# SyncE's table numbers packed by two, its waits grouped, and a ring of eight y buffers in the expert stage

## The reference

```python
h = embed(x); h = conv31(h) + bias                  # 8 x 512 tokens, 256 channels
h = h + attention(layernorm(h))                     # 16 heads of 64, linear attention
h = h + experts(layernorm(h))
# experts, for 4096 tokens (xf) and 8 experts, four 256 wide and four 512 wide
probs = sigmoid(xf @ router_w.T)
topw, sel = top_k(probs, 2); topw = topw / (topw.sum(-1, keepdims=True) + 1e-20)
h = square(relu(einsum('td,edw->tew', xf, W1e)))
y = einsum('tew,ewd->ted', h, W2e)
out = einsum('ted,te->td', y, combine)              # combine: topw at the two chosen experts
```

## Time and profile before

| | before |
|---|---|
| median of 3 runs | 714.23 us (714.22 to 716.38) |
| the profiled execution | 714.98 us, its span 713.3 us |
| PE busy | 631.3 us (89%), 5032 matmuls |
| DVE busy | 468.4 us (66%) |
| ACT busy | 306.8 us (43%) |
| POOL busy | 321.1 us (45%), of it 71 adds (L1748) 111.8 us |
| row loads of the expert stage (L1715) | 71, 129.0 KB each, median 2.1 us from issue to landing |
| adds (L1748) | 71, median 4.0 us from issue to landing |

### The profile page before, as it was taken

The page is one execution under the profiler, slowest core; times in us unless marked ns, Lnnn a source line. Parts: engine busy times, 40 slices in busy tenths (PEclk is TensorE's granted clock), DMA queues, the critical chain, the costliest instruction groups (busy, mean ns, idle before and its releaser), DMA issues.

```text
span 713.3 us, 15773 instructions
## 1 busy us (share of the span) xinstructions
PE 631.3 (89%) x5032; PEld 546.0 (77%) x5032; DVE 468.4 (66%) x1219; ACT 306.8 (43%) x669; POOL 321.1 (45%) x292
## 2 busy tenths in 40 slices
PE   6988479999999999999999999615999999988881
PEld 6988357788887887878878787504999999888781
DVE  6466494877879778797897866764444555554450
ACT  2560135334453353633535327422545555555551
POOL 6340351330833717427165171752354544476574
PEclk9999698999999999999999999856999999999996
DMA  6550982010111201102010020423355445576664
GB/s 225 190 124 7 230 301 62 2 59 2 61 60 39 82 1 60 60 24 97 1 61 31 17 75 3 169 93 101 62 87 80 78 76 83 79 116 108 107 100 45
DMA packets 37215, 58.11 MB, mean 81 GB/s; under 512 B 5726, under 2 KB 31066, under 8 KB 36506
## 3 DMA queue, kind: packets, MB, share of 16 engines
q1 hardware_dynamic: 21282, 35.08, 16.9%
q0 software_dynamic: 14160, 20.13, 15.7%
q10 hardware_dynamic: 1672, 1.57, 0.7%
HBM read 28.30 MB, written 27.42 MB: 78 GB/s over the span
## 4 chain that ended last, share of the span: by engine, by line
PE 77%; DMA 8%; DVE 6%; issue 3%; POOL 2%; ACT 1%; SPq 1%; DVEq 0%; ACTq 0%; POOLq 0%
PE bank L1427 26%; PE bank L1859 16%; PE bank L1500 7%; DMA out<-y,token_at 7%; PE bank L1470 5%; PE bank L1456 4%; PE bank L1875 2%; PE bank L1488 2%; PE bank L546 2%; PE bank L547 2%; PE bank L567 2%; PE bank L1849 2%; PE bank L529 1%; PE bank L1418 1%; PE bank L1556 1%
## 5 line engine op out<-in xcount | busy, mean ns | idle before, releaser
L1748 POOL DMA_INDIRECT out<-y,token_at x71 | 111.8, 1575 | 108.3 <-SPq L1727 107.1
L886 POOL DMA_INDIRECT queue_d<-row,slot x56 | 59.7, 1066 | 129.0 <-DVE slot L1253 114.2
L1817 DVE SCALAR_TENSOR_TENSOR act_w<-relu,queue_rows 128x512 f32<-128x512 f32 (+1 forms) x71 | 44.6, 628 | 98.2 <-ACT relu L1765 52.0
L1427 PE MATMUL bank<-xt_hi,w_first 128*128 128x512 f32 x256 | 94.8, 416 | 0.9 <-DVE second_half L1091 0.9
L1427 PE MATMUL bank<-w_first,xt_hi 128*128 128x512 f32 x256 | 84.7, 412 | 3.1 <-DVE xt_lo L1081 2.3
L877 POOL TENSOR_TENSOR second_half<-second_half,q_inv 128x512 f32<-128x512 f32 x64 | 64.9, 1042 | 42.0 <-DVE q_inv L1100 41.9
L945 ACT ACTIVATE k_exps<-bank,k_negmax 128x512 f32<-128x512 f32 x64 | 44.2, 691 | 73.8 <-DVE k_negmax L1107 73.6
L937 ACT ACTIVATE second_half<-second_half 128x512 f32<-128x512 f32 x64 | 40.3, 632 | 74.3 <-DVE second_half L1091 74.3
L1859 PE MATMUL bank<-w_hi,a_hi 128*128 x214 | 65.9, 308 | 0.8 <-issue 0.5
L1427 PEld LDWEIGHTS bank<-w_first,xt_hi 128*128 128x128 f32 x256 | 46.2, 192 | 19.6 <-issue 6.8
L1859 PE MATMUL bank<-w_lo,a_hi 128*128 x214 | 59.8, 280 | 0.0
(11 more groups left out here) (201 smaller groups left out, 1583.8 us busy)
## 6 DMA issues: line engine op xcount, KB each, us to landing
queue_rows<-queue_d SPq DMA_DIRECT2D x71, 129.0 KB, 2.1
store<-in_L_ffn_w SPq DMA_DIRECT2D x4, 1536.0 KB, 8.6
out<-res SPq DMA_DIRECT2D x8, 512.0 KB, 2.9
h_d<-store SPq DMA_DIRECT2D x6, 512.0 KB, 9.0
h_in<-h_d SPq DMA_DIRECT2D x6, 512.0 KB, 4.1
windows<-taps_d SPq DMA_DIRECT2D x4, 512.0 KB, 5.8
wqk<-in_L_attn_w_qkv SPq DMA_DIRECT2D x1, 2048.0 KB, 13.5
out<-y,token_at POOLq DMA_INDIRECT x71, 4.0
```

The costliest lines, as they stand in the source:

```text
L886: pool.indirect_dma_start(out=queue_d, in_=row_of(b)[:, t, c, :], in_offset=None, out_offset=bass.IndirectOffsetOnAxis(ap=slot[:, TT * c + ...
L1427: last = nc.tensor.matmul(o, a, c, start=(n == 1), stop=(n == 3 * len(pairs)))
L1748: pool.indirect_dma_start(out=out, in_=y[:, j % RING, :], in_offset=None, compute_op=ALU.add, out_offset=bass.IndirectOffsetOnAxis(ap=toke ...
L1817: nc.vector.scalar_tensor_tensor(out=act_w[:, u % 2, 0:width], in0=relu[:, u % 2, 0:width], scalar=rows[:, u, DIM:DIM + 1], in1=relu[:, u ...
```

## The change

1. **Two tiles in a word.** VectorE now packs, for two tiles, the tile number in `queue_d` (9 bits, row / 128) and one bit for "another expert than the tile before" into one number, `step_of` (36 numbers in place of 72 + 72). SyncE loads one number for two tiles and takes it apart with shifts and masks in registers; `row_of` and `apart` are gone.
2. **The clamp comes first.** `expert_f` is clamped to 7 before neighbours are compared, so a filler tile behind expert 7 no longer counts as another expert.
3. **RING = 8.** Eight buffers of `y` and eight `added` semaphores. `take_y` waits for the add of tile j-8, and `allow` has to look at seven adds before, not three. In the first round of the ring that is now tiles 0 to 7, so the plain limit of 16 holds for adds of tiles 0 to 7.
4. **Waits grouped.** The seven waits have at most two limits (two rounds of the ring), so the sum in a register is made once for each round, and `sp_passed` is raised at most once for a tile.

```diff
--- before.py
+++ after.py
@@ -70,6 +70,9 @@
 TOPK = 2
 QROWS = TOKENS + P
 FILLER_ROW = EXPERTS * QROWS
+STEPS = 2
+ROW_BITS = 9
+STEP_BITS = ROW_BITS + 1
 ROW = DIM + 2
 
 TILES = TOKENS * TOPK // P + EXPERTS - 1
@@ -78,8 +81,9 @@
 SLOTS = 8
 TABLE = -(-TILES // SLOTS) * SLOTS
 FILLERS = TABLE - TOKENS * TOPK // P
+LAST_TILE = (FILLER_ROW + FILLERS * P) // P - 1
 TURN = 2
-RING = 4
+RING = 8
 TOTAL_W = sum(WIDTHS)
 
 
@@ -129,10 +133,8 @@
         self.end = sbuf("end", [P, EXPERTS])
         self.end_i = sbuf("end_i", [P, EXPERTS], I32)
         self.tile_no = sbuf("tile_no", [1, TABLE])
-        self.row_of = sbuf("row_of", [1, TABLE], I32)
+        self.step_of = sbuf("step_of", [1, TABLE // STEPS], I32)
         self.word_of = sbuf("word_of", [1, TABLE // SLOTS], I32)
-
-        self.apart = sbuf("apart", [1, TABLE], I32)
         self.consts, self.filler_ready, self.ends_ready, self.filled, self.chain, self.ready = (sem(n) for n in (
             "table_consts", "filler_ready", "ends_ready", "filled", "table_chain", "table_ready"))
 
@@ -1357,15 +1359,17 @@
                                         ALU.mult))
         chained(nc.vector.tensor_reduce(start_f, passed, AX, ALU.add))
         chained(nc.vector.tensor_tensor(start_f, table.tile_no[:], start_f, ALU.subtract))
-        chained(nc.vector.tensor_scalar(start_f, start_f, float(P), None, ALU.mult))
-        chained(nc.vector.scalar_tensor_tensor(out=start_f, in0=expert_f, scalar=float(QROWS), in1=start_f,
+        chained(nc.vector.scalar_tensor_tensor(out=start_f, in0=expert_f, scalar=float(QROWS // P), in1=start_f,
                                             op0=ALU.mult, op1=ALU.add))
-        chained(nc.vector.tensor_copy(table.row_of[:], start_f))
+        chained(nc.vector.tensor_scalar(expert_f, expert_f, float(EXPERTS - 1), None, ALU.min))
 
         chained(nc.vector.memset(differs[:, 0:1], 0.0))
         chained(nc.vector.tensor_tensor(differs[:, 1:], expert_f[:, 1:], expert_f[:, 0:TABLE - 1], ALU.not_equal))
-        chained(nc.vector.tensor_scalar(table.apart[:], differs, 16.0, None, ALU.mult))
-        chained(nc.vector.tensor_scalar(expert_f, expert_f, float(EXPERTS - 1), None, ALU.min))
+        chained(nc.vector.scalar_tensor_tensor(out=start_f, in0=differs, scalar=float(2 ** ROW_BITS), in1=start_f,
+                                            op0=ALU.mult, op1=ALU.add))
+        pairs = start_f.rearrange("p (n u) -> p n u", u=STEPS)
+        chained(nc.vector.scalar_tensor_tensor(out=table.step_of[:], in0=pairs[:, :, 1], scalar=float(2 ** STEP_BITS),
+                                               in1=pairs[:, :, 0], op0=ALU.mult, op1=ALU.add))
 
         pairs = expert_f.rearrange("p (n u) -> p n u", u=2)
         chained(nc.vector.scalar_tensor_tensor(out=word2, in0=pairs[:, :, 1], scalar=float(EXPERTS),
@@ -1706,35 +1710,47 @@
         attention_left(sp)
 
 
-        def row_at(j):
-            return sp.value_load(table.row_of[0:1, j:j + 1], min_val=0, max_val=FILLER_ROW + (FILLERS - 1) * P)
-
-        def load(j, at):
+        def steps_from(j):
+
+            n = j // STEPS
+            return sp.value_load(table.step_of[0:1, n:n + 1], min_val=0, max_val=2 ** (STEPS * STEP_BITS) - 1)
+
+        def load(j, steps):
             if j >= SLOTS:
                 sp.wait_ge(row_used, j - SLOTS + 1)
-            sp.dma_start(rows[:, j % SLOTS], queue_d[bass.ds(at, P), :]).then_inc(rows_in[j % SLOTS], 16)
-
-        def allow(j):
-
+            at = (steps >> (STEP_BITS * (j % STEPS))) & (2 ** ROW_BITS - 1)
+            at = nc.s_assert_within(at, 0, LAST_TILE, skip_runtime_bounds_check_because="the table numbers queue_d's tiles")
+            sp.dma_start(rows[:, j % SLOTS], queue_d[bass.ds(at * P, P), :]).then_inc(rows_in[j % SLOTS], 16)
+
+        def wait_landed(tiles, turn, apart16):
+
+            for b in tiles:
+                if b // RING == turn:
+                    sp.wait_ge(added[b % RING], apart16 + 16 * turn if turn > 0 else 16)
+
+        def allow(j, steps):
+
+            apart16 = (steps >> (STEP_BITS * (j % STEPS) + ROW_BITS - 4)) & 16
+            earlier = range(max(0, j - RING + 1), j)
             sp.wait_ge(y_ready, j + 1)
-            if j >= RING:
-                differs16 = sp.value_load(table.apart[0:1, j:j + 1], min_val=0, max_val=16)
-            for before in range(max(0, j - RING + 1), j):
-                if before < RING:
-                    sp.wait_ge(added[before % RING], 16)
-                else:
-                    wait_apart(sp, added[before % RING], differs16 + 16 * (before // RING), sp_passed)
+            if earlier and earlier[0] // RING < (j - 1) // RING:
+                wait_landed(earlier, earlier[0] // RING, apart16)
+                sp.sem_inc(sp_passed, 1)
+            if earlier:
+                wait_landed(earlier, (j - 1) // RING, apart16)
             sp.sem_inc(may_add, 1)
 
-        first_rows = [row_at(j) for j in range(SLOTS)]
+        words = [steps_from(j) for j in range(0, SLOTS, STEPS)]
         sp.wait_ge(table.filled, 16 * (EXPERTS + 3))
         sp.wait_ge(queued, 16 * TOPK * TT * BATCHES)
         for j in range(SLOTS):
-            load(j, first_rows[j])
+            load(j, words[j // STEPS])
         for j in range(TILES):
             if j + SLOTS < TILES:
-                load(j + SLOTS, row_at(j + SLOTS))
-            allow(j)
+                if j % STEPS == 0:
+                    words.append(steps_from(j + SLOTS))
+                load(j + SLOTS, words[(j + SLOTS) // STEPS])
+            allow(j, words[j // STEPS])
 
     def gpsimd(pool):
         attention_left(pool)
```

## The result

The changed kernel takes 708.74 us (median of 10 runs, 706.27 to 713.0), the kernel before, beside it, 716.38 (10 runs, 713.67 to 718.72): ratio 0.9912, with a 95% interval of 0.989 to 0.9935. Two more sets of runs of the same pair gave 0.9911 (0.9883 to 0.994) and 0.9902 (0.9875 to 0.993). The profiled execution took 708.07 us with a span of 706.4; 708.8 was forecast for it, and 708.0 for the median. That forecast counted from three runs of the kernel before, with a median of 714.23; the difference forecast was 6.2 us, and the three sets give 6.3, 6.4 and 7.0 by their ratios.

A forecast was written before the change was run, and what follows sets the result against it. SyncE's program was taken to pace the narrow part's adds, with expert changes on top. Terms: -6.3 + 0.1 = -6.2 us, so 708.8 for the profiled execution and 708.0 for the median, range 706.2 to 711.2.

The forecast's parts named there:

- SyncE's 1.48: SyncE's program per tile after the change: 1.48 us in place of 2.04, bounds 1.1 to 1.76.
- Rival (1): SyncE gains nothing, releases stay 2.04 us apart: gain 3.3 to 4.4 us, time 710.4; chance 0.08.
- GpSimd's floor: Adds of y into out: GpSimd's own shortest pace, 1.86 us per add, becomes the adds' pace.
- Rival (4): Adds following at once occupy GpSimd for 2.19 us, not 1.86: 1.2 us later than now, 715.4; chance 0.04.
- The walk: Adds followed from tile 44 to the last: tile 70 at 699.1 us against 705.40, a gain of 6.3.
- rival (2): TensorE's late y at the end isn't the ring's doing, tile 68's y stays at 696.29: 710.2 us; chance 0.08.
- The filler's wait: Wait ahead of tile 69, the first filler tile, goes through the earlier clamp: 2.2 us gained.
- rival (5): The wait ahead of the first filler tile stays: + 2.2 us, 710.2; chance 0.02.
- The forecast of 4.1 for the rest: Adds in the narrow part: backlog that no longer builds, 4.1 of the 6.3 us gained.
- The serial start: Tiles 1 to 8 serial in place of 1 to 4: row loads keep 3.0 us of slack, nothing lost.
- Rival (3): Row loads come late if serial steps average over 4.9 us: 714 us or slower; chance 0.04.
- 0.1 us lost (0 to 0.2): Start of the stage: a mask added ahead of tile 0's row load costs 0.1 us.

The follow-up runs named there:

- The two ring experiments: Changed kernel with RING = 4: 708.91 us, ratio 0.9903; kernel before with RING = 8 and nothing else: 721.94 us, ratio 1.0097, both to the kernel before.
- the two runs beside which the kernel before took 725.65 us: Changed kernel with the branch's two sides exchanged: 719.87 us, ratio 0.993; changed kernel without the branch, code fixed at build: 716.1 us, ratio 0.9872.
- turns of four: Changed kernel with TURN = 4, one branch for four tiles in place of two: 719.78 us, ratio 1.0068 to the kernel before.
- the exchanged sides: Changed kernel with the branch's sides exchanged, narrow code first and reached without a jump: 719.87 us, ratio 0.993 to the kernel before.

## Why the prediction was right, step by step

**What bounded the kernel.** That SyncE's program paced the narrow part and the ring only handed it on was the reading of the earlier trace rows. The two ring experiments show it from both sides.

**SyncE's 1.48.** Measured 1.53 as a mean (1.24 and 1.77 in turn), inside the bounds of 1.1 and 1.76. The forecast needed no more of it than "under 1.86". The release stands 0.51 us behind the end of y where 0.6 was taken. Rival (1) needed releases 2.04 apart, and is out.

**GpSimd's floor.** 1.86 us, 21 times. Rival (4), adds that lengthen when packed: the median stayed 1557 ns with 21 of them close together in the narrow part. The longest went from 1892 to 1997 ns, but it was 2064 and 2088 in two kernels with the old program, so that isn't the packing. It is out. The rule of the Trainium skill behind it (SBUF — State Buffer, "SBUF: two separate sides", VectorE's two-port operations shut GpSimd out) shows no effect here that an add's length would tell; whether VectorE's operations beside the adds are of that kind no view here shows.

**The walk.** Forecast and measured, adds: tile 8 536.3 and 535.34; 44 641.0 and 640.18; 45 645.5 and 644.57; 50 654.8 and 653.87; 51 659.2 and 658.54; 56 668.5 and 667.84; 57 673.0 and 672.40; 68 695.3 and 694.60; 70 699.1 and 698.32. The forecast stands 0.6 to 1.0 late all along, since this execution's stage began earlier (tile 0 at 499.40, where 500.33 and the 0.1 of the start make 500.43); from tile 0 to 70 the forecast makes 198.7, and 198.92 came. Landings at changes plus start: 4.39, 4.67 and 4.56, where 4.46 was taken each time. y took 18.14, 17.85 and 18.57 us for eight tiles, where 18.11 was taken; rival (2) is out.

**The filler's wait.** 2.2 forecast; 2.2 by P of the run without the clamp, so rival (5) is out. The forecast of 4.1 for the rest holds as 3.9.

**The serial start.** Nothing forecast, nothing seen (P 198.83 without it). Eight steps didn't use up the slack at tile 17; sixteen did. Rival (3) is out.

**The start was mis-sized.** "0.1 us lost (0 to 0.2)" was the step that failed. It counted one mask on the way to tile 0's load and left out what stands on the way to tile 1's, and what the clock would do: 1.5, 1.6 and 1.2 us in three runs of the changed kernel, of which some 0.4 go with SyncE's start and the rest with the clock. That the net time came out right all the same is in part luck: in the profiled pair 2.4 us ahead of the first row load, which nothing in the forecast had, more than made up for it. By the ratios the change gained 6.3 to 7.0 us (6.7 to 7.6 by the medians themselves), as much as or more than P alone (6.2), though with the 1.5 taken off it P leaves only 4.7. The some 2 us between 4.7 and the ratios these profiles don't place. Ahead of the first row load the code is the same, and executions of it vary: the first row load of the kernels with the changed table lies between 482.9 and 487.7 us (without the two runs beside which the kernel before took 725.65 us), of the kernels with the old one between 483.95 and 485.93. GpSimd's first write to a queue, about 178 us in, varies already as much (176.7 to 181.0). A profile each is too little to tell whether the change moves this part too.

**One expectation of the experiments failed, and half of another.** That of turns of four read 337 ns as the price of any branch, from kernels that all jump over two tiles. It also left out that TensorE's clock could fall while it stands still. That of the exchanged sides had two theories. The first, that nothing changes in the narrow part, held. The second compared medians over groups with one record to a pair and with two.

## What to carry over

When an engine without arithmetic of its own, such as SyncE, serves others, count its program per step start to start, loads of numbers first: 0.55 us each here, against 0.07 for a register operation. Before buffers are added, ask who makes them wait; a ring that waits may only hand on another engine's pace, and more buffers can lengthen the very program that sets it, by 6.9 us here (0.97% of 715.2). A wait that is caught up in the middle costs in full at the end, where nothing catches it up: the filler's wait was 2.2 us of 6.2 for one moved instruction.

## What the hardware showed beside this

- A branch of TensorE around two tiles of code: 0.31 us in records if its first side runs (28 records, 4.4 us, 14 pairs of wide tiles), 0.32 if the second does; around four tiles 0.43 (one of 0.97 us among them) and 1.02, at most 2.7. Taken out with the unused side it was worth 0.75 us a pair.
- A landing did not grow as the adds came closer: the median is 4.1, 4.0 and 3.9 us in three runs of the changed kernel, the longest 5.6, 5.9 and 5.0; with the old program it is 4.0 in all three, the longest 5.3, 5.6 and 5.2.
- SyncE's queue shows 0.5 us of nothing between the register operation behind a row load and the next, where shifts and masks follow at once (483.91 to 484.44 us, in the changed kernel); what it does there no view tells.
- TensorE's clock rose 5.2 to 5.9 us after work began in five executions and 7.1 to 8.4 in nine, with nearly the same work, and that was worth more than the change's own step there.
- With branches around four tiles TensorE's clock fell to half three times in the narrow part, for 10.2 us in all, each time when TensorE had just stood still for 1.5 us or more of 2. In the changed kernel, where no single wait of TensorE's products there is over 1.3 us, the clock stayed at full speed from 493.6 to 698.4 us.
